# Expert outputs stored from ScalarE's DMA queue and read back in two sets, with eight extra products ahead of the combine

## The chip, the cores and the metric

The kernel runs on one core of a Trainium2 chip. The metric is the device time of one execution in microseconds: the median of three runs before the change is 980.36 us (977.6 to 984.06).

## The reference, cut to what matters

The program is a small vision tower: patch embedding of 64 images (37 tokens of 192 values each), causal linear attention, a soft mixture of 64 experts, a neighbourhood attention and a routed mixture of 8 experts. The change touches only the soft mixture. All of it is in 32-bit floats.

```python
d = softmax(logits, axis=tokens)            # dispatch weights, 64 experts, one slot each
c = softmax(logits, axis=experts)           # combine weights
xs = einsum('bmd,bmn->bnd', xn, d)          # one input row per image and expert
h  = gelu(einsum('bnd,ndh->bnh', xs, w1) + b1)   # w1: 64 x 192 x 768
ys = einsum('bnh,nhd->bnd', h, w2) + b2          # w2: 64 x 768 x 192
y  = einsum('bnd,bmn->bmd', ys, c)          # combine: every token mixes the 64 rows of its image
```

Each expert makes 64 rows of 192 values, one for each image. The combine needs, for a tile of three images, the rows of all 64 experts for these images.

## The kernel before

Five engines run five programs that meet at semaphores only. Within an engine, and within the DMA queue of an engine, all is issued in the written order. The stages follow each other: embedding, attention, dispatch, experts, combine, neighbourhood attention, routed experts. The experts and the combine are the place of the change.

**Experts.** The 64 experts are worked through as 32 pairs (expert p on output partitions 0 to 63, expert p + 32 on 64 to 127). For each pair SyncE's (SP's) queue loads two blocks of 1152 KB: w1 at L1067, w2 at L1070. They go into a ring of six places (`RING`; tiles `w1s`/`w1l` and `w2s`/`w2l`). TensorE (PE) makes the hidden product of pair s (L1177, L1181), the transposes of pair s - 1 (L1192) and the output product of pair s - 2 (L1203). ScalarE (ACT) copies half of the hidden rows (L1106, `copy_h`), applies gelu to the pair before (L1111), and copies the output of the pair before that into one of four tiles `eo` (L1118, `output`); VectorE (DVE) copies the other half and adds b1.

**Where the outputs go.** For the first 27 pairs (`DIRECT`) SP stores the two 64 x 192 halves of `eo` to `ys` in DRAM (L1078). These stores stand in the same queue as the loads: after the loads of pair p + 6. For pairs 27 to 31 SP copies from `eo` straight into the combine's tiles, one expert at a time (L1081, three transfers for an expert, each into one partition). Once the stores of pairs 0 to 26 have landed, six transfers of 27 rows each bring these back from DRAM (L1091, L1092).

**The combine's tiles.** They lie in ring places that are free by then: `e1` (in `w1l`) holds images 0 to 20 of expert n in partition n, and images 21 to 41 in partition 64 + n; `e2` (in `w2l`) holds images 42 to 63 in partition n, and b2 in partitions 64 to 127 (L1083, one load of 64 rows). A row of `e1` is 21 x 192 values (16,128 bytes), one of `e2` 22 x 192 (16,896 bytes). So in the trace L1091 reads as `w1l<-ys`, L1092 as `w2l<-ys`, and L1081 as `w1l<-eo` and `w2l<-eo`.

**Combine.** PE transposes the combine weights of 22 tiles (L1243, L1244), ACT copies them out (L1218), and then PE waits at L1248 for all rows of `e1` and `e2` before its 44 products (L1258, L1259). VectorE adds each to `h` (L1226). The next stage starts behind them.

Of the kernel before, what the change touches and what calls it, by code (L numbers as in the profile page):

```python
# [14 lines left out]
B, C_IN, IMG, PATCH = 64, 3, 96, 16  # L15
# [5 lines left out]
GB = 3  # L21
TP = GB * S
PARTS = ((0, TP // 16 * 16), (TP // 16 * 16, TP))
T = 22
# [4 lines left out]
NE, HID = 64, 768  # L29
HB = HID // 128  # L30
NPAIR = NE // 2
RING = 6
EARLY = 2
EOB = 4
DIRECT = 27
HALF_HID = HID // 2
QKW = 2 * NH * DH
VGW = NH * DH + ED
# [79 lines left out]
def tower(nc, ins, rows_out):  # L118
    with ExitStack() as ctx:
        scope = [ctx]  # L120

        def sb(name, shape, dt=F32):
            return scope[-1].enter_context(nc.sbuf_tensor(name, shape, dt))
# [9 lines left out]
        def sem(name):  # L133
            return ctx.enter_context(nc.semaphore(name))

        bank = [ctx.enter_context(nc.psum_tensor(f"bank{i}", [128, 512], F32)) for i in range(8)]
# [9 lines left out]
        ident = identity[:]  # L146
# [26 lines left out]
        xy = sb("xy", [128, 2, NE, B])  # L173
# [4 lines left out]
        w1s = [sb(f"w1s{q}", [128, 3 * HID]) for q in range(EARLY)]  # L178
        w2s = [sb(f"w2s{q}", [128, 2, HB, ED]) for q in range(EARLY)]
# [88 lines left out]
        eo = [sb(f"eo{b}", [128, ED]) for b in range(EOB)]  # L268
# [3 lines left out]
        e1 = w1l[:, 0:2].rearrange("p s (t d) -> p (s t) d", d=ED)  # L272
        e2 = w2l[:, 0:2].rearrange("p s e j d -> p (s e j) d")
        cTs = [w1l[:, 2:4].rearrange("p s n -> p (s n)"), w2l[:, 2].rearrange("p e j d -> p (e j d)")]

        def cT(t):
            k, at = t // CTN, t % CTN * 2 * TP
            return cTs[k][:, at:at + 2 * TP].rearrange("p (c q) -> p c q", c=2)
# [87 lines left out]
        ys_of = ys.rearrange("(n m) d -> n m d", n=NE)  # L366
# [60 lines left out]
        s_eoo = [sem(f"slot_output_out{b}") for b in range(EOB)]  # L427
# [18 lines left out]
        s_w1 = [sem(f"w1_in{q}") for q in range(RING)]  # L446
        s_w2 = [sem(f"w2_in{q}") for q in range(RING)]
        s_dh = sem("expert_hidden_product")
# [4 lines left out]
        s_dy = sem("expert_output_product")  # L453
        s_do = sem("expert_output_stored")
# [3 lines left out]
        s_el = sem("expert_rows_in")  # L458
# [45 lines left out]
        s_h = sem("h_updated")  # L504
# [552 lines left out]


        def experts_sp(sp):
            for s in range(NPAIR + RING):  # L1060
                q = s % RING
                if s < NPAIR:
                    if s == EARLY:
                        sp.wait_ge(s_h, 2 * T)
                    if s >= RING:
                        sp.wait_ge(s_dh, s - RING + 1)
                    sp.dma_start(w1s[q][:], ins["w1"][s]).then_inc(s_w1[q], 16)  # L1067
                    if s >= RING:
                        sp.wait_ge(s_dy, s - RING + 1)
                    sp.dma_start(w2s[q][:], ins["w2"][s]).then_inc(s_w2[q], 16)  # L1070
                p = s - RING
                if p >= 0:
                    b = p % EOB
                    sp.wait_ge(s_do, p + 1)
                    for e in range(2):
                        n = p + e * NPAIR
                        if p < DIRECT:
                            sp.dma_start(ys_of[n], eo[b][e * B:(e + 1) * B]).then_inc(s_eoo[b], 16)  # L1078
                        else:
                            for to, lo, hi in places(n):  # L1080
                                sp.dma_start(to, eo[b][e * B + lo:e * B + hi]).then_inc(s_eoo[b], 16)  # L1081
                if p == DIRECT:
                    sp.dma_start(e2[NE:2 * NE, 0:T], ins["b2"].rearrange("n (t d) -> n t d", d=ED)).then_inc(s_el, 16)  # L1083
                if p == DIRECT + 1:
                    for r in range(DIRECT - EOB, DIRECT):
                        sp.wait_ge(s_eoo[r % EOB], rows_out_by(r))
                    for k in range(2):
                        n = slice(k * NPAIR, k * NPAIR + DIRECT)
                        for g in range(2):
                            to = slice(g * NE + k * NPAIR, g * NE + k * NPAIR + DIRECT)  # L1090
                            sp.dma_start(e1[to, 0:T - 1], ys_of[n, g * (T - 1):(g + 1) * (T - 1)]).then_inc(s_el, 16)  # L1091
                        sp.dma_start(e2[n, 0:T], ys_of[n, 2 * (T - 1):B]).then_inc(s_el, 16)  # L1092

        def places(n):
            return ((e1[n:n + 1, 0:T - 1], 0, T - 1), (e1[NE + n:NE + n + 1, 0:T - 1], T - 1, 2 * (T - 1)), (e2[n:n + 1, 0:T], 2 * (T - 1), B))

        def rows_out_by(p):
            return sum(16 * (2 if r < DIRECT else 2 * GB) for r in range(p % EOB, p + 1, EOB))

        def experts_act(act):  # L1100
            def copy_h(p):
                b = p % 2
                act.wait_ge(s_dh, p + 1)
                if p >= 2:
                    act.wait_ge(s_dt, p - 1)
                nc.scalar.copy(eh[b][:, 0:HB // 2], hidden_bank(b, 0)).then_inc(s_dc[0], 1)  # L1106

            def gelu(p):
                b = p % 2
                act.wait_ge(s_db, p + 1)  # L1110
                nc.scalar.activation(eg[b][:], eg[b][:], ACT.Gelu).then_inc(s_dg, 1)  # L1111

            def output(p):
                b = p % 2
                act.wait_ge(s_dy, p + 1)
                if p >= EOB:
                    act.wait_ge(s_eoo[p % EOB], rows_out_by(p - EOB))
                nc.scalar.copy(eo[p % EOB][:], bank[6 + b][:, 0:ED]).then_inc(s_do, 1)  # L1118

            for s in range(NPAIR + 2):  # L1120
                if s < NPAIR:
                    copy_h(s)
                if 0 <= s - 1 < NPAIR:
                    gelu(s - 1)
                if s >= 2:
                    output(s - 2)

        def hidden_bank(b, part):
            return bank[2 * b + part][:, 0:HALF_HID].rearrange("p (j k) -> p j k", j=HB // 2)
# [104 lines left out]
        def combine_pe(pe):  # L1234
            for part in range(2):
                pe.wait_ge(s_dc[part], NPAIR)

            def transpose_c(t):
                pe.wait_ge(s_ecw, t + 1)
                if t >= 4:  # L1240
                    pe.wait_ge(s_eTa, t - 3)
                spread = cw[t % CB][:].rearrange("p g n -> p (g n)")
                nc.tensor.transpose(bank[t % 4][:, 0:TP], spread[:, 0:128], ident[0:TP, 0:TP])  # L1243
                nc.tensor.transpose(bank[t % 4][:, TP:2 * TP], spread[:, 128:4 * NE], ident[0:TP, 0:TP]).then_inc(s_eT, 1)  # L1244

            for t in range(T):
                transpose_c(t)
            pe.wait_ge(s_el, 16 * (1 + 2 * GB))  # L1248
            for b in range(EOB):
                pe.wait_ge(s_eoo[b], rows_out_by(NPAIR - EOB + b))  # L1250
            pe.wait_ge(s_db, NPAIR)
            pe.wait_ge(s_do, NPAIR)
            pe.wait_ge(s_eTa, T)

            def product(t):
                if t >= 4:
                    pe.wait_ge(s_h, 2 * T + t - 3)
                nc.tensor.matmul(bank[4 + t % 4][0:TP, 0:ED], cT(t)[:, 0], e1[:, t, :], start=True, stop=False)  # L1258
                nc.tensor.matmul(bank[4 + t % 4][0:TP, 0:ED], cT(t)[:, 1], e2[:, t, :], start=False, stop=True).then_inc(s_ey, 1)  # L1259

            for t in range(T):
                product(t)
# [738 lines left out]
        @block.sync  # L2001
        def _(sp):
            embed_sp(sp)
            sp.wait_ge(s_cbi, 32)
            experts_sp(sp)
            near_sp(sp)
            routed_sp(sp)
# [7 lines left out]
        @block.scalar  # L2015
        def _(act):
            embed_act(act)
            attention_act(act)
            dispatch_act(act)
            experts_act(act)  # L2020
            combine_act(act)
            near_act(act)
            near_act2(act)
            route_act(act)
            routed_act(act)
# [12 lines left out]
        @block.tensor  # L2038
        def _(pe):
            embed_pe(pe)  # L2040
            attention_pe(pe)
            dispatch_pe(pe)
            experts_pe(pe)
            combine_pe(pe)
            near_pe(pe)
            route_pe(pe)
            routed_pe(pe)
# [106 lines left out]
```

## Time and profile before

| | us |
|---|---|
| runs before | 977.6, 980.36, 984.06 |
| profiled execution, its own time | 982.76 |
| span from its first to its last instruction | 980.9 |
| experts, first hidden product to last output product | 263.4 to 436.6 |
| transposes of the combine weights | 436.5 to 442.2 |
| products of the combine | 458.5 to 475.6 |

The profiled execution lies 2.4 us above the median of the three runs and inside their range. Its mean granted TensorE clock is 0.912. TensorE is busy in 88% of the span; there is no second engine near that. The 16 DMA engines are 90% busy or more only in some stretches, and the longest of these is the experts' stage.

Times in all rows are microseconds from the start of the span, unless ns is written. "DMA share" is the mean busy share of the 16 DMA engines.

### The profile page before, as it was taken

The numbers are of one execution on the slowest core, as the hardware profiler recorded it, in microseconds if no ns is written. First come the engines' busy times: TensorE is split into PE (matmuls) and PEld (weight loads), VectorE is DVE, ScalarE is ACT, GpSimd is POOL, SyncE is SP. The second block draws the span as 40 slices with busy tenths as digits, with TensorE's granted clock in tenths as the row PEclk, the third lists the DMA queues.
The fourth block names the chain that finished last, engine by engine and source line by source line (L and its number), as shares of the span: only waits on it lengthen the run. The fifth ranks groups of instructions, "written<-read, shape, count | busy, mean of one in ns | idle before, by whom it ended". The sixth has DMA issues, their size and how long they took to land. (4 is left out here: it accounts for less than half of the span.)

```text
span 980.9 us, 17879 instructions
## 1 busy us (share of the span) xinstructions
PE 858.5 (88%) x6209; PEld 621.5 (63%) x6209; DVE 455.5 (46%) x1520; ACT 318.1 (32%) x904; POOL 280.1 (29%) x242
## 2 busy tenths in 40 slices
PE   6899999899999999893997999977465999999991
PEld 6787888676466655463854777757453666666661
DVE  6864565548443322241654688836781222222220
ACT  2544333237433332240042566633101121221210
POOL 1540000000000000000233455530027488888444
PEclk9999999799899999996997899985556999999996
DMA  8992000270089999982500000002005354455222
GB/s 265 281 329 97 2 2 2 81 305 2 23 320 423 423 422 423 425 263 70 175 1 1 1 2 0 1 2 53 24 24 140 79 105 104 92 101 104 39 24 25
DMA packets 59881, 128.93 MB, mean 131 GB/s; under 512 B 26334, under 2 KB 42256, under 8 KB 50112
## 3 DMA queue, kind: packets, MB, share of 16 engines
q1 hardware_dynamic: 29858, 118.61, 33.3%
q0 software_dynamic: 29952, 9.36, 7.0%
q8 instruction: 45, 0.74, 0.3%
q14 instruction: 26, 0.21, 0.1%
HBM read 115.76 MB, written 11.49 MB: 130 GB/s over the span
## 5 line engine op out<-in xcount | busy, mean ns | idle before, releaser
L1831 POOL DMA_INDIRECT out_dram<-yr,put x48 | 105.7, 2203 | 58.3 <-issue 35.4
L1286 POOL MEMSET xg<- 96x74 f32 x1 | 0.2, 157 | 406.9 <-PE bank L1259 406.9
L1818 POOL DMA_INDIRECT zr<-z_rows,take x48 | 66.6, 1388 | 84.6 <-issue 84.6
L1895 PE MATMUL bank<-zTa,w 128*128 128x372 f32 x256 | 90.0, 496 | 0.8 <-DVE zTb L1969 0.8
L1978 DVE TENSOR_TENSOR hT<-sg,bank 128x372 f32<-128x372 f32 x64 | 31.8, 538 | 107.5 <-ACT sg L1939 63.1
L1895 PEld LDWEIGHTS bank<-zTa,w 128*128 128x128 f32 x256 | 47.5, 194 | 38.2 <-ACT sg L1939 8.4
L1143 DVE COPY eh<-bank 128x384 f32<-128x384 f32 x32 | 17.8, 558 | 110.6 <-PE bank L1181 110.6
L1909 PE MATMUL bank<-w2r,hT 128*124 128x192 f32 x384 | 66.1, 329 | 0.8 <-DVE hT L1978 0.8
L1939 ACT ACTIVATE sg<-bank 128x372 f32<-128x372 f32 x64 | 27.3, 478 | 115.4 <-PE bank L1900 115.4
L1909 PEld LDWEIGHTS bank<-w2r,hT 128*124 128x124 f32 x384 | 61.9, 187 | 3.8 <-issue 3.8
L1327 POOL TENSOR_TENSOR nl<-nl,nr 111x1036 f32<-111x1036 f32 x22 | 42.1, 1914 | 61.7 <-DVE nr L1437 61.7
L1463 ACT ACTIVATE nl<-nl,nn 111x259 f32<-111x259 f32 x88 | 43.9, 500 | 48.1 <-DVE nn L1430 48.1
L1572 PE MATMUL bank<-kT,qx 96*111 (+1 forms) x176 | 53.5, 434 | 1.4 <-DVE nm L1428 1.3
L800 PE MATMUL bank<-wtok_c,xT 128*111 128x192 f32 x264 | 46.3, 331 | 5.7 <-DMA xT<-in_xT_dram 4.1
L1900 PE MATMUL bank<-zTb,w 64*128 64x372 f32 x256 | 48.7, 498 | 0.0
L800 PEld LDWEIGHTS bank<-wtok_c,xT 128*111 128x111 f32 x264 | 42.1, 176 | 9.9 <-issue 6.5
L1428 DVE CUSTOM_DVE_ANT_0 nl<-bank,bias 111x259 f32<-111x259 f32 x88 | 36.6, 424 | 15.4 <-issue 15.0
L1203 PE MATMUL bank<-w2l,eg 128*64 128x192 f32 x480 | 43.4, 330 | 0.0
L1111 ACT ACTIVATE eg<-eg 128x768 f32<-128x768 f32 x32 | 27.0, 845 | 41.0 <-DVE eg L1154 41.0
L1106 ACT COPY eh<-bank 128x384 f32<-128x384 f32 x32 | 15.3, 479 | 69.3 <-PE bank L1181 69.3
L1900 PEld LDWEIGHTS bank<-zTb,w 64*128 64x128 f32 x256 | 22.0, 186 | 24.6 <-issue 17.0
L1572 PEld LDWEIGHTS bank<-kT,qx 96*111 96x111 f32 x176 | 29.7, 195 | 12.0 <-issue 4.2
(298 smaller groups left out, 1798.4 us busy)
## 6 DMA issues: line engine op xcount, KB each, us to landing
w1l<-in_w_dram SPq DMA_DIRECT2D x20, 1152.0 KB, 16.3
w2l<-in_w_dram SPq DMA_DIRECT2D x20, 1152.0 KB, 16.9
w1s<-in_w_dram SPq DMA_DIRECT2D x12, 1152.0 KB, 15.5
w2s<-in_w_dram SPq DMA_DIRECT2D x12, 1152.0 KB, 15.1
w<-in_w_dram SPq DMA_DIRECT2D x8, 1024.0 KB, 8.0
xt<-in_x_dram SPq DMA_DIRECT2D x22, 336.0 KB, 8.0
xT<-in_xT_dram SPq DMA_DIRECT2D x22, 333.0 KB, 7.4
w2r<-in_w2r_dram SPq DMA_DIRECT2D x8, 384.0 KB, 4.1
```

The lines of the kernel that those rows point to most:

```text
L800: last = nc.tensor.matmul(bank[2 + q % 2][0:TP, 0:ED], xT[q][:, k, :], wtok_c[:, k, :], start=(k == 0), stop=(k == KC - 1))
L1203: last = nc.tensor.matmul(bank[6 + b][e * B:(e + 1) * B, 0:ED], eg[b][:, j, e, :], w2s[q][:, e, j, :], start=(j == 0), stop=(j == HB - 1))
L1327: nc.gpsimd.tensor_tensor(nl[q][:], nl[q][:], nr[b][:].unsqueeze(2).to_broadcast([TP, NHN, KW]), ALU.mult).then_inc(s_nw, 1)
L1428: nc.vector.tensor_tensor_reduce(nl[q][:, head, :], bank[1 + head % 2][0:TP, 0:KW], bias[v][:, head, :], 1.0, -3.0e38, ALU.add, ALU.max, n ...
L1463: last = nc.scalar.activation(nl[q][:, head, :], nl[q][:, head, :], ACT.Exp, bias=nn[b][:, head:head + 1], accum_out=nsum[b][:, head:head ...
L1572: nc.tensor.matmul(bank[1 + head % 2][0:TP, 0:KW], qx[q % 2][:, head, :], kT[:, bass.ds(first, KW)], start=True, stop=True).then_inc(s_nS, 1)
L1818: nc.gpsimd.indirect_dma_start(zr[b][:, j, :], None, z_rows, bass.IndirectOffsetOnAxis(ap=take[:, k:k + 1], axis=0), bounds_check=NROW - 1 ...
L1831: nc.gpsimd.indirect_dma_start(rows_out, bass.IndirectOffsetOnAxis(ap=put[:, k:k + 1], axis=0), yr[e % 2][:, j, :], None, bounds_check=OUT ...
L1895: nc.tensor.matmul(bank[to + 2 * part + half][:, 0:HS], w13[b][:, 0, at:at + 128], zTa[b][:, half * HS:(half + 1) * HS], start=True, stop= ...
L1900: nc.tensor.matmul(bank[to + 2 * part + half][:, 0:HS], w13[b][rows, 1, at:at + 128], zTb[b][rows, :], start=False, stop=True).then_inc(s_ ...
L1909: last = nc.tensor.matmul(bank[2 + j % 2][0:SP_, 0:ED], hT[:, m, j * SP_:(j + 1) * SP_], w2r[b][:, m, :], start=(m == 0), stop=(m == EH // ...
L1978: nc.vector.tensor_tensor(hT[:, m, half * HS:(half + 1) * HS], sg[half][:], bank[4 * (m % 2) + 2 + half][:, 0:HS], ALU.mult).then_inc(s_hT, 1)
```

## The change

Three things change. ACT issues the stores of all 32 pairs, each right behind its copy to `eo`, after waiting for that copy; SP issues no stores and no direct copies any more. SP reads the rows back in two sets of six transfers: pairs 0 to 27 (28 rows a transfer) and pairs 28 to 31 (4 rows a transfer), each set after a wait for the stores of its last four pairs; b2 is loaded once pair 27's output product is done. And PE issues eight products of the identity with 256 columns of `xy`, a tile that lies in SBUF already, between the transposes and its wait; their result is not used.

```diff
-DIRECT = 27
+FIRST = 27
...
         def experts_sp(sp):
-            for s in range(NPAIR + RING):
+            for s in range(NPAIR):
                 q = s % RING
...
+                if s == EARLY:
+                    sp.wait_ge(s_h, 2 * T)
+                if s >= RING:
+                    sp.wait_ge(s_dh, s - RING + 1)
+                sp.dma_start(w1s[q][:], ins["w1"][s]).then_inc(s_w1[q], 16)
+                if s >= RING:
+                    sp.wait_ge(s_dy, s - RING + 1)
+                sp.dma_start(w2s[q][:], ins["w2"][s]).then_inc(s_w2[q], 16)
+                if s == NPAIR - 1:
+                    sp.wait_ge(s_dy, FIRST + 1)
                     sp.dma_start(e2[NE:2 * NE, 0:T], ins["b2"].rearrange("n (t d) -> n t d", d=ED)).then_inc(s_el, 16)
...
+            for first, last in ((0, FIRST), (FIRST + 1, NPAIR - 1)):
+                for p in range(last + 1 - EOB, last + 1):
+                    sp.wait_ge(s_eoo[p % EOB], rows_out_by(p))
+                for k in range(2):
+                    read_back(sp, slice(k * NPAIR + first, k * NPAIR + last + 1))
+
+        def read_back(sp, n):
+            for g in range(2):
+                to = slice(g * NE + n.start, g * NE + n.stop)
+                sp.dma_start(e1[to, 0:T - 1], ys_of[n, g * (T - 1):(g + 1) * (T - 1)]).then_inc(s_el, 16)
+            sp.dma_start(e2[n, 0:T], ys_of[n, 2 * (T - 1):B]).then_inc(s_el, 16)
 
         def rows_out_by(p):
-            return sum(16 * (2 if r < DIRECT else 2 * GB) for r in range(p % EOB, p + 1, EOB))
+            return 32 * (p // EOB + 1)
...
                 nc.scalar.copy(eo[p % EOB][:], bank[6 + b][:, 0:ED]).then_inc(s_do, 1)
+                act.wait_ge(s_do, p + 1)
+                for e in range(2):
+                    act.dma_start(ys_of[p + e * NPAIR], eo[p % EOB][e * B:(e + 1) * B]).then_inc(s_eoo[p % EOB], 16)
...
-            pe.wait_ge(s_el, 16 * (1 + 2 * GB))
-            for b in range(EOB):
-                pe.wait_ge(s_eoo[b], rows_out_by(NPAIR - EOB + b))
+            for _ in range(8):
+                nc.tensor.matmul(bank[4][:, 0:256], ident, xy[:, 0, 0:4, :].rearrange("p n m -> p (n m)"), start=True, stop=True)
+            pe.wait_ge(s_el, 16 * (1 + 4 * GB))
```

ACT in the experts' steady state, one pair and the start of the next, before:

```order
L1106 COPY eh<-bank 128x384
L1111 ACTIVATE eg<-eg 128x768
L1118 COPY eo<-bank 128x192
L1106 COPY eh<-bank 128x384
L1111 ACTIVATE eg<-eg 128x768
```

and with the change:

```order
L1094 COPY eh<-bank 128x384
L1099 ACTIVATE eg<-eg 128x768
L1106 COPY eo<-bank 128x192
L1109 DMA ys<-eo 64x192 x2
L1094 COPY eh<-bank 128x384
```

Two DMA issues now stand on ACT between the output copy of one pair and the hidden copy of the next.

SP from the last loads to the end of the combine's transfers, before (from the stores of pair 26):

```order
L1078 DMA ys<-eo 64x192
L1081 DMA w1l<-eo 1x21x192 [waits expert_output_stored]
L1081 DMA w1l<-eo 1x21x192
L1081 DMA w2l<-eo 1x22x192
L1081 DMA w1l<-eo 1x21x192 x2
L1081 DMA w2l<-eo 1x22x192
L1083 DMA w2l<-in_b_dram 64x4224
...
L1091 DMA w1l<-ys 27x4032 [waits slot_output_out1,slot_output_out2,slot_output_out0,slot_output_out3]
L1091 DMA w1l<-ys 27x4032
L1092 DMA w2l<-ys 27x4224
```

and with the change (from the last load of w2):

```order
L1069 DMA w2s<-in_w_dram 128x2304 [waits expert_output_product]
L1072 DMA w2l<-in_b_dram 64x4224 [waits expert_output_product]
L1082 DMA w1l<-ys 28x4032 [waits slot_output_out2,slot_output_out3,slot_output_out1,slot_output_out0]
L1082 DMA w1l<-ys 28x4032
L1083 DMA w2l<-ys 28x4224
L1082 DMA w1l<-ys 28x4032 x2
L1083 DMA w2l<-ys 28x4224
L1082 DMA w1l<-ys 4x4032 [waits slot_output_out2,slot_output_out3,slot_output_out1,slot_output_out0]
L1082 DMA w1l<-ys 4x4032
L1083 DMA w2l<-ys 4x4224
```

The 30 direct copies of pairs 27 to 31 are gone from SP; six transfers of four rows, behind one more wait, take their place.

## Rows read from the trace of the kernel before

**Rows 1.** Waits of PE: waiter and releaser, total us, times, longest.
```profile
PE bank L1258 <- DMA w2l<-eo: 16.3, 1, 16.3
```

**Rows 2.** Windows: each engine's busy us and instructions, PEclk, DMA share, GB/s.
```profile
300.00:360.00 60.00, 60.00 (x554) 36.30 (x550) 19.29 (x37) 19.69 (x36) 0.00 (x0) 1.00 1.02 424
360.00:426.00 66.00, 57.63 (x510) 32.59 (x506) 17.38 (x33) 18.41 (x35) 0.00 (x0) 1.00 1.01 421
426.00:434.00 8.00, 7.67 (x74) 5.13 (x76) 2.60 (x5) 2.20 (x4) 0.00 (x0) 1.00 0.84 177
434.00:448.00 14.00, 8.19 (x74) 6.33 (x70) 4.79 (x14) 7.84 (x26) 0.00 (x0) 0.95 0.57 183
450.00:456.00 6.00, 0.00 (x0) 0.00 (x0) 0.00 (x0) 0.00 (x0) 0.00 (x0) 0.50 0.28 37
452.00:456.00 4.00, 0.00 (x0) 0.00 (x0) 0.00 (x0) 0.00 (x0) 0.00 (x0) 0.50 0.19 27
456.00:458.50 2.50, 0.00 (x0) 0.00 (x0) 0.00 (x0) 0.00 (x0) 0.00 (x0) 0.50 0.00 0
```

**Rows 3.** Timeline, one late pair: start, duration, engine, line [idle before <-releaser].
```profile
392.05 0.48 ACT L1106 COPY eh<-bank 128x384 f32<-128x384 f32 x1 [2.57 <-PE bank L1181]
...
393.88 0.84 ACT L1111 ACTIVATE eg<-eg 128x768 f32<-128x768 f32 x1 [1.35 <-DVE eg L1154]
...
394.94 0.32 ACT L1118 COPY eo<-bank 128x192 f32<-128x192 f32 x1 [0.21 <-PE bank L1203]
...
396.13 3.88 SPq L1078 DMA_DIRECT2D ys<-eo  x2
...
398.65 0.48 ACT L1106 COPY eh<-bank 128x384 f32<-128x384 f32 x1 [3.39 <-PE bank L1181]
...
400.06 0.64 SPq L1067 DMA_DIRECT2D w1s<-in_w_dram  x1
```

**Rows 4.** Line L1078, issue of one store: ns min/median/max, first and last start.
```profile
L1078 SPq DMA_DIRECT2D ys<-eo x54: 445/597/3665, 275.5 to 414.7; - x54
```

**Rows 5.** Timeline from the last stores to the combine's first product.
```profile
408.39 6.89 SPq L1078 DMA_DIRECT2D ys<-eo  x4
...
424.79 0.55 SPq L1083 DMA_DIRECT2D w2l<-in_b_dram  x1
425.29 0.32 ACT L1118 COPY eo<-bank 128x192 f32<-128x192 f32 x1 [0.21 <-PE bank L1203]
...
433.26 0.68 SPq L1091 DMA_DIRECT2D w1l<-ys  x2
...
436.60 0.32 ACT L1118 COPY eo<-bank 128x192 f32<-128x192 f32 x1 [1.78 <-PE bank L1203]
...
441.93 0.26 PE L1244 MATMUL bank<-identity,cw 111*128 111x111 f32 x1
...
449.07 0.77 SPq L1081 DMA_DIRECT2D w2l<-eo  x1
458.50 0.44 PEld L1258 LDWEIGHTS bank<-w1l 128*111 128x111 f32 x2 [16.53 <-issue]
```

**Rows 6.** DMA issues: tiles, queue, count, KB each, median us to landing.
```profile
w1l<-ys SPq DMA_DIRECT2D x4, 425.2 KB
...
w2l<-ys SPq DMA_DIRECT2D x2, 445.5 KB
...
z_rows<-zk SPq DMA_DIRECT2D x1, 67.5 KB, 3.2
```

**Rows 7.** Windows of the combine, columns as in Rows 2.
```profile
446.00:450.00 4.00, 0.00 (x0) 0.00 (x0) 0.00 (x0) 0.00 (x0) 0.00 (x0) 0.58 0.48 151
458.50:462.00 3.50, 3.47 (x11) 3.39 (x12) 0.91 (x3) 0.00 (x0) 0.00 (x0) 0.50 0.00 0
462.00:464.00 2.00, 2.00 (x9) 1.95 (x8) 0.75 (x4) 0.00 (x0) 0.00 (x0) 0.57 0.00 0
```

**Rows 8.** Line L1002, earlier products of the identity with 256 columns: ns min/median/max.
```profile
L1002 PE MATMUL bank<-w1s,identity x60: 379/379/741, 190.0 to 215.0; 128*128 128x256 f32 x60
```

More of the change, by code:

```diff
@@ L1059, in experts_sp @@
         def experts_sp(sp):
-            for s in range(NPAIR + RING):
+            for s in range(NPAIR):
                 q = s % RING
[L1062 to L1082, printed above, removed]
-                    sp.dma_start(e2[NE:2 * NE, 0:T], ins["b2"].rearrange("n (t d) -> n t d", d=ED)).then_inc(s_el, 16)
[L1084 to L1092, printed above, removed]
@@ L1094, in places @@
-        def places(n):
-            return ((e1[n:n + 1, 0:T - 1], 0, T - 1), (e1[NE + n:NE + n + 1, 0:T - 1], T - 1, 2 * (T - 1)), (e2[n:n + 1, 0:T], 2 * (T - 1), B))
+                if s == EARLY:
[6 more added lines that the diff above has]
+                sp.dma_start(w2s[q][:], ins["w2"][s]).then_inc(s_w2[q], 16)
```

## The prediction

> **What bounds the kernel now.** I read the waits of PE first, because PE is busy almost all the time and what it waits for is what can be saved. One wait belongs to this change: 16.3 us before the combine's first product, for transfers into the combine's tiles [rows 1]. Next I read the windows by stage [rows 2]. From 300 to 426 us the DMA engines are at a share of 1.01 to 1.02 and move 421 to 424 GB/s. From 360 us on PE is busy in only 57.63 of 66 us while the DMA engines never rest: the loads of the expert weights set the pace there. After 426 us the picture turns round. The DMA share falls to 0.57 and the rate to 183 GB/s, then to 37 and 27 GB/s, and 2.5 us without any DMA pass before PE starts. So the end of the stage is set by a chain of transfers that are slow without filling the engines. The timeline has its links [rows 5]: the last stores of pairs up to 26 are issued by 415.3 us (408.39 + 6.89), SP issues the read-back at 433.26, the last output is copied at 436.60 to 436.92, SP issues its last direct copy at 449.07, PE starts at 458.50. PE has had nothing to do since 442.2 (441.93 + 0.26).
>
> **Loads: no gain.** SP loses an issue of 3.88 us for each pair's stores [rows 3], and the next w1 load can be issued that much earlier. But the bytes of loads and stores up to 426 us stay the same, and at a share of 1.01 an earlier issue only lengthens the queue. I take 0. If the share fell below 1 there, this would be a gain of at most the 8.4 us that PE stands idle between 360 and 426 us (66 - 57.63) [rows 2]; nothing in the rows points to that.
>
> **ACT: no cost, with a limit.** ACT now issues two stores after each output copy and waits for that copy first. No row has a DMA issued by ACT. The nearest is the same store on SP: 0.445 us at least, 0.597 median, 3.665 at most [rows 4]. So a pair costs ACT 0.9 to 7.3 us. I take the median, 1.2, since the high values come when SP's own queue is full of loads, and ACT's queue holds none. What waits behind it is the next hidden copy, and ACT is idle for 3.39 us before that [rows 3]. Over 360 to 426 us ACT is idle 47.6 us (66 - 18.41) [rows 2]; at 6.6 us a pair (398.65 - 392.05) [rows 3] that is ten pairs and 4.7 us a pair. So 1.2 us is covered, and up to 4.7 us could be. At the end, ACT's issue for pair 31 delays its copies of the combine weights by 1.2 us, so the transposes end near 443.4. PE waits much longer than that.
>
> **First set.** Pair 27's output copy ends at 425.61 [rows 5]; the two issues end at 426.8. Landing: the low end is 3.2 us, a lone store of similar size [rows 6]; the high end is 18 us, what lies between the last stores' issue at 415.3 and the read-back that waited for them at 433.26 [rows 5], behind loads. I take 5 us, near the low end because no load stands ahead in ACT's queue, but the engines are still at 0.84 [rows 2] with the last loads and b2. With about 1 us for issue and first bytes, the set runs from 433: where it ran before. It is 28/27 of 4 x 425.2 + 2 x 445.5 KB [rows 6], that is 2,688 KB or 2.75 MB. At 183 GB/s [rows 2] that is 15.0 us, to 448. The low end: a share of 0.57 is 9.1 engines, and 27 rows can be dealt evenly to nine; if 28 rows go to fourteen at the same 20 GB/s an engine, 9.8 us. I take 15.0, since b2 with 64 rows shows that more engines need not mean more bytes: 177 GB/s at a share of 0.84 [rows 2].
>
> **Second set.** It waits for pair 31's stores: copied at 436.92 [rows 5], issued at 438.1, landed between 441.3 (3.2 us) and 456.1 (18 us). I take about 448, because they share the engines with the first set; so the set starts at about 448.5, behind the first. Its six transfers have 4 x 16,128 or 4 x 16,896 bytes, together 393 KB. Four rows can be dealt to four engines only, which is my inference from the nine above. The low end is four engines at the load stage's pace (424/16 = 26.5 GB/s each): 3.7 us. The high end is the slowest stretch of the direct copies, 27 GB/s [rows 2]: 14.6 us. I take 37 GB/s [rows 2], 10.6 us, because those copies too write to very few partitions at a time, and so are nearest to four. That ends at 459.1.
>
> This is where a rule of the Trainium skill speaks against the change. The rows show that transfers into few partitions are slow for the engines they keep busy: 27 GB/s at a share of 0.19 is 9 GB/s an engine, against 26.5 in the loads [rows 2]. The page SBUF — State Buffer, section Door 1: The DMA port swizzle, says that bandwidth depends on how many of 16 ports the partitions reach, at about 27.2 GB/s each, and puts partitions 28 to 31 and 60 to 63 on one port. By that page the second set takes about 14.5 us where the sum has 10.6; the trace's 27 GB/s for single partitions agrees.
>
> **The eight products.** At 0.379 us each [rows 8] they last 3.0 us, from 443.4 to 446.4, and delay nothing. The clock fell at 446.6 before (a mean of 0.58 over 446 to 450 [rows 7]), 4.4 us after PE went idle at 442.2, and the combine began at half of 2.4 GHz: 0.50, then 0.57 up to 464 [rows 7]. That costs about 2.6 us, half of the first 5.2. With the start that I get, PE is idle for some 15 us behind the eight products; the clock falls all the same. I take 0, with a gain of 2.6 if the gap stays shorter than it was when the clock fell.
>
> **Sum.** 459.1 plus 2.5 us from the last bytes to PE [rows 2] is 461.6, against 458.5: +3.1 us, and all later stages shift with it. The profiled execution of 982.76 us becomes about 986. It lies 2.4 us above the median of 980.36, so for a median I forecast 980.4 + 3.1, 983.5, and round to **984 us**.
>
> **Rivals.**
> - *Faster: the second set is not slow.* All low ends at once: first set from 431 to 440.8, second from 441.8 to 445.5, PE at 448.0, 10.5 us earlier, and 2.6 more from the clock, since PE then idles only 1.6 us: about 967. For it: no more single-partition copies, fourteen engines instead of nine. Against it: the low rates after 426 us, in three kinds of transfer. Half way, with the first set at 15 us and the second at 3.7, PE starts at about 455, 4 us earlier. Chance 0.17, of which 0.08 over 1%.
> - *The rows go one transfer after another at the slowest rate.* Second set 14.6 us, PE at 465.6, +7.1: about 987. It is the skill's rule, told above. Chance 0.12.
> - *Slower: pair 31's stores land late.* If they take 18 us, as the last stores did before, they land at 456.1, the set runs from 456.6 to 467.2, PE starts at 469.7, +11.2: about 992. For it: ACT issues them while the engines work through the first set's long rows. Against it: the 18 us came behind loads. It costs over 1% from a landing of 16.6 us on; below 9.9 us it costs nothing beyond the forecast. Chance 0.16.
> - *Slower: ACT's issues are held up in the loads.* From 4.7 us a pair on, ACT becomes the bound; at 7.3 us it is 2.6 us a pair over some ten pairs, +26: about 1010. Chance 0.05.
> - *The eight products do not do what they are there for.* This is inside the forecast: without a gap under 4.4 us the clock is as before.
>
> **Numbers.** The forecast, +3.1 with its own range of -3 to +9 us (977 to 989), has chance 0.50. About 1%, or 9.8 us, is what a measurement of this kernel can tell from no change. Faster by over 1%: 0.08. Slower by over 1%: 0.15 from the late landing, 0.05 from ACT, together 0.20. Within: 0.72. The range of 970 to 994 reaches half of the fast case and the late landing, and leaves out ACT's and the full fast case.
>
> **What would show it.** The loads' DMA share stays at 1.0 up to about 426 us and PE's hidden products keep their spacing: the loads' step is right. ACT's idle time before the hidden copy shrinks by about 1.2 us; if it goes to zero in most pairs, ACT's step was wrong. The first 28-row transfer is issued near 432, the first 4-row one between 441 and 449. In the stretch of the second set the rate is 27 to 40 GB/s; if it is over 80, the faster rival holds. PE's first combine product stands near 461, at a granted clock of 0.50. The prediction is wrong above all if the rate of the second set is, or if the stores on ACT's queue land much sooner or later than I took.

## The result: 0.45% slower, as forecast in size, by terms that missed in both directions

| | before | after |
|---|---|---|
| median of 15 runs each, us | 984.38 (977.6 to 987.67) | 988.31 (983.14 to 992.18) |
| ratio, with 95% interval | | 1.0045 (1.0026 to 1.0064) |
| profiled execution, its own time | 982.76 | 988.92 |
| span | 980.9 | 987.1 |
| ACT's last output copy to the combine's first product | 436.60 to 458.53: **21.93** | 435.74 to 460.71: **24.97** |

The kernel became 4.4 us slower (0.0045 x 984.4; 2.6 to 6.3). The forecast was +3.1 us and 984 us. 4.0 of the 4.3 us between 984 and 988.31 lie in the base: 15 runs of the kernel before have a median of 984.38, the three that the forecast began from had 980.36. So 988.31 is still inside the forecast's own 977 to 989, by 0.7 us. The last line of the table is the change's own price in the profile: +3.04 us. Everything below is measured in this distance, because the stage itself begins earlier or later from one execution to the next: the first hidden product stands between 258.0 and 268.6 us in the profiles of this document.

**The profile after.** PE's wait into the combine, as waiter and releaser, total us, times, longest; it answers [rows 1]. The releaser is now the second read-back (`w2l<-ys`):

```profile
PE bank L1249 <- DMA w2l<-ys: 14.9, 1, 14.9
```

The windows, columns as in [rows 2]: the load stage, the first set, the second set, and the combine's beginning.

```profile
300.00:360.00 60.00, 59.62 (x550) 35.98 (x544) 19.29 (x37) 19.38 (x36) 0.00 (x0) 1.00 1.02 423
360.00:426.00 66.00, 58.15 (x512) 32.94 (x514) 17.37 (x33) 18.36 (x34) 0.00 (x0) 1.00 1.02 422
...
434.00:448.00 14.00, 10.68 (x82) 8.65 (x78) 4.87 (x14) 7.16 (x24) 0.00 (x0) 1.00 0.83 196
446.00:450.00 4.00, 0.00 (x0) 0.00 (x0) 0.00 (x0) 0.00 (x0) 0.00 (x0) 0.93 0.16 43
...
450.10:459.90 9.80, 0.00 (x0) 0.00 (x0) 0.00 (x0) 0.00 (x0) 0.00 (x0) 0.50 0.22 40
460.70:466.00 5.30, 5.29 (x17) 5.14 (x18) 1.60 (x5) 0.00 (x0) 0.00 (x0) 0.50 0.00 0
```

Up to 426 us nothing has changed: share 1.02, 422 GB/s, the same PE load. From 434 to 448 us the share rose from 0.57 [rows 2] to 0.83, 13.3 engines on average (0.83 x 16) in place of 9.1, but the rate only from 183 to 196 GB/s. In the second set some four engines (0.22 x 16 is 3.5) move 40 GB/s: by the packet records (the trace has start, length and size of every DMA packet) its 24 rows run from 450.18 to 459.90 us, 9.7 us. The clock fell and PE begins the combine at 0.50, as before.

The timeline of a late pair, answering [rows 3]: start, duration, engine, line, [idle before <-releaser].

```profile
386.24 0.48 ACT L1094 COPY eh<-bank 128x384 f32<-128x384 f32 x1 [2.57 <-PE bank L1172]
...
389.12 0.32 ACT L1106 COPY eo<-bank 128x192 f32<-128x192 f32 x1 [0.21 <-PE bank L1194]
389.47 1.70 ACTq L1109 DMA_DIRECT2D ys<-eo  x2
...
392.02 0.48 ACT L1094 COPY eh<-bank 128x384 f32<-128x384 f32 x1 [2.58 <-PE bank L1172]
```

The two issues lie inside the 2.58 us in which ACT waits for PE anyway; these hidden copies follow each other at 5.78 us.

The timeline from the first set's issue to the combine, answering [rows 5]:

```profile
431.70 0.77 SPq L1082 DMA_DIRECT2D w1l<-ys  x2
...
435.74 0.32 ACT L1106 COPY eo<-bank 128x192 f32<-128x192 f32 x1 [1.95 <-PE bank L1194]
...
436.08 1.10 ACTq L1109 DMA_DIRECT2D ys<-eo  x2
...
442.15 3.63 PE L1240 MATMUL bank<-xy,identity 128*128 128x256 f32 x16
...
449.32 0.58 SPq L1082 DMA_DIRECT2D w1l<-ys  x2
...
460.71 0.98 PE L1249 MATMUL bank<-w1l 128*111 128x192 f32 x2 [14.92 <-DMA w2l<-ys]
```

SP issues the second set at 449.32, when pair 31's stores have landed: 12.1 us after ACT finished issuing them (436.08 + 1.10). The DMA issues from 428 to 461 us (KB each, median us from issue to landing; [rows 6] has those of before) say the same of the last six stores:

```profile
ys<-eo ACTq DMA_DIRECT2D x6, 48.0 KB, 11.8
```

The span grew by 6.2 us, 3 more than the distance. Before the tail the profile after is 0.9 us ahead, so the other 4 us arise behind the combine, in stages that the change doesn't touch. The windows of the neighbourhood attention show a part of them: before,

```profile
545.00:550.00 5.00, 4.97 (x22) 3.87 (x21) 2.77 (x13) 2.92 (x10) 2.13 (x2) 0.60 0.00 0
550.00:556.00 6.00, 5.84 (x60) 4.74 (x61) 4.24 (x24) 3.32 (x12) 2.38 (x2) 1.00 0.00 0
```

and after:

```profile
545.00:550.00 5.00, 5.00 (x22) 4.40 (x22) 2.81 (x14) 2.16 (x9) 1.30 (x2) 0.50 0.02 3
550.00:556.00 6.00, 6.00 (x37) 4.38 (x36) 3.09 (x18) 2.28 (x9) 2.13 (x2) 0.57 0.00 0
```

The clock came back near 549 before (a mean of 0.60 over 545 to 550) and near 555 after (0.57 over 550 to 556), 4 us more than the stage is late, and 37 products were done where 60 had been. In the granted-clock records this stretch at 0.50 lasts 27.3 us here (527.9 to 555.2), 23.9 us before (525.2 to 549.0), and 23.9 us again in the first and the eighth experiment, which have the same two sets. So nothing ties it to the change; it is most likely of this one execution. The ratio's interval covers 3.1 us without it.

### The profile page after: what moved, and what is told of

Same layout as the page of the kernel before. It is cut to its first block and busy times, and to the rows that moved or that the text cites. A ratio compares the mean times of both kernels' runs of the same rounds, so it can differ in the third digit from the quotient of the medians.

```text
span 987.1 us, 17897 instructions
## 1 busy us (share of the span) xinstructions
PE 865.5 (88%) x6225; PEld 626.6 (63%) x6225; DVE 455.4 (46%) x1520; ACT 318.0 (32%) x904; POOL 279.8 (28%) x242
## 5 line engine op out<-in xcount | busy, mean ns | idle before, releaser
L1930 ACT ACTIVATE sg<-bank 128x372 f32<-128x372 f32 x64 | 27.3, 478 | 115.6 <-PE bank L1891 115.6
```

## The experiments

Each distance is from the start of ACT's last output copy to the combine's first product, as in the table above; the expectations count from the end of the last output product, 0.04 us earlier. Ratios are to runs of the kernel before on the same chip; these had medians of 985.17, 984.45 and 985.76 us in the three groups of runs (1 to 4, 5 to 8, 9 to 11). My theory after the result: the chain is pair 31's stores, then a second set slow because it writes to few partitions; the products do nothing. The main rivals: the stores' place on ACT costs something by itself, and the read-back is limited by all engines together, wherever it writes.

**1. Without the eight products.**

```diff
-            for _ in range(8):
-                nc.tensor.matmul(bank[4][:, 0:256], ident, ...)
```

> The changed kernel without the eight products of the identity. Theory (the second set's chain sets the start of the combine, the clock falls with or without the products): the combine's first product stays at 460.7 us, within 0.5, after 15 us of waiting without the products' 3.6 us, again at a granted clock of 0.50; against the kernel before the ratio stays at 1.0045, within 0.003. Rival (the products hold something up, or keep the clock for part of the combine): the time moves by 2 us or more against the changed kernel.

Ratio 1.0026 (1.0 to 1.0053); 442.26 to 466.73, 24.47 us. The products neither cost nor gain anything that can be seen. The first product itself stands at 466.73 us and not at 460.7, because the whole stage began 5.9 us later.

**2. Only the stores moved to ACT.** The kernel before, with the stores of pairs 0 to 26 issued by ACT; direct copies and the read-back of 27 rows stay on SP.

```diff
...
                 nc.scalar.copy(eo[p % EOB][:], bank[6 + b][:, 0:ED]).then_inc(s_do, 1)
+                if p < DIRECT:
+                    act.wait_ge(s_do, p + 1)
+                    for e in range(2):
+                        act.dma_start(ys_of[p + e * NPAIR], ...)
```

> The kernel before with one part of the change: ACT issues the stores of pairs 0 to 26, the direct copies of pairs 27 to 31 and the one read-back of 27 rows stay on SP. Theory (the loads are bound by the DMA engines, so an earlier issue gives nothing; only the end of the stage counts): the last output product ends where it did, 436.6 us within 1; the read-back is issued some 1 to 3 us earlier than at 433.3, and the combine starts 0 to 3 us before 458.5; ratio 0.997 to 1.0. Rival (ACT's issues or a second queue cost the loads something): the last output product ends later by 2 us or more and the time is above that of before.

Ratio 0.9993 (0.997 to 1.0016); 440.99 to 461.63, 20.64 us: 1.3 us less than before. The last output product ends at 440.95 and not at 436.6, which was the rival's first sign; but the first hidden product is 4.7 us later too, and from one to the other the experts take 172.9 us (173.2 before). The time is not above that of before, so the rival is out. The move to ACT alone is free. With the first run, which leaves out the products, the 3 us come from what becomes of the last pairs and of the read-back.

**3. One set.** All 32 rows are read back behind pair 31's stores.

```diff
-            for first, last in ((0, FIRST), (FIRST + 1, NPAIR - 1)):
+            for first, last in ((0, NPAIR - 1),):
```

> The changed kernel with a single read-back of all 32 rows, issued once pair 31's stores have landed: 3.1 MB in place of the second set's 0.39 MB at the end. Theory (rows into few partitions are slow, and 32 rows spread over eight times as many partitions run at the rate of the first set, about 196 GB/s, so eight times the bytes cost less than twice the time): pair 31's stores land within 5 us as nothing else moves then (441 to 443), the read-back takes 15 to 16 us, and the combine starts at 459 to 461, the same as with two sets; ratio 1.001 to 1.006. Rival A (bytes over the engines' full rate count): 3.1 MB at 424 GB/s take 7.4 us, and the combine starts near 452. Rival B (the second set's rate holds per byte, 0.39 MB in 8.7 us): the combine starts far later, beyond 500.

Ratio 0.9973 (0.9951 to 0.9994); 437.07 to 456.58, **19.51 us**: 5.5 less than with two sets, and 2.4 less than before. The timeline, and the DMA issues from 428 to 461 us:

```profile
437.42 1.10 ACTq L1109 DMA_DIRECT2D ys<-eo  x2
439.98 1.53 SPq L1082 DMA_DIRECT2D w1l<-ys  x2
...
456.58 0.98 PE L1249 MATMUL bank<-w1l 128*111 128x192 f32 x2 [9.46 <-DMA w2l<-ys]
```

```profile
ys<-eo ACTq DMA_DIRECT2D x6, 48.0 KB, 2.4
```

```profile
442.00:454.00 12.00, 5.12 (x30) 4.12 (x28) 0.91 (x3) 3.40 (x10) 0.00 (x0) 0.84 1.02 229
```

With no read-back beside them the same six stores land in 2.4 us (median) where they took 11.8, and pair 31's within 1.5 us of their issue (438.52 to 439.98). So reading back early is what delays the stores that the second set waits for. The expectation of 459 to 461 missed this by 2.4 us, by 3.8 us counted from the last copy: it gave the stores up to 5 us, and they took 1.5. And 3.1 MB take 14.9 us (440.95 to 455.84 by the packet records), where the 0.39 MB of the second set alone took 9.7.

**4. One set from two queues.** As the third, but ACT issues the two transfers into partitions 64 to 127.

```diff
-            for g in range(2):
-                sp.dma_start(e1[to, 0:T - 1], ...)
+            sp.dma_start(e1[n, 0:T - 1], ...)
...
+                act.dma_start(e1[to, 0:T - 1], ys_of[n, T - 1:2 * (T - 1)])
```

> As the single read-back of 32 rows, but the two transfers into partitions 64 to 127 are issued by ACT, the four into partitions 0 to 63 by SP, at the same time. Theory (each half of the partitions has its own limit near 100 to 110 GB/s per 32 rows' worth of time, and one queue works through its transfers one after another, so only one half is busy at a time): both halves run together, the read-back takes the time of four transfers of the six, about 10 us, and the combine starts at 453 to 456; ratio 0.996 to 1.0. Rival (the limit is the DRAM side or all engines together at about 196 GB/s): two queues change nothing, 15 to 16 us, start at 459 to 461.

Ratio 0.9955 (0.9929 to 0.9981); 436.29 to 455.59, 19.30 us. The start at 455.6 lies inside what the theory expected, but not for its reason: the read-back took 14.9 us (440.16 to 455.10 by the packet records), as long as from one queue, and not the 10 us that it wanted. So a second queue gains nothing here, and no run shows a limit of 100 to 110 GB/s for each half. What does limit the rows is left open by this run: of the first 128 rows 63 are ACT's, so both halves were written at once, but the records do not name the engine of a row. (ACT waits for the last stores before it copies the combine weights, so the transposes end at 446.93; PE waits longer than that.)

**5. One set, rows spread over the partitions.** Row 32k + i moves from partition 64g + 32k + i to 4i + 2k + g, so that a transfer reaches every fourth partition and not 32 neighbours. b2 follows, in two transfers, and DVE spreads the combine weights in two operations a tile.

```diff
-                to = slice(g * NE + n.start, g * NE + n.stop)
-                sp.dma_start(e1[to, 0:T - 1], ...)
+                sp.dma_start(e1[rows_of(n, g), 0:T - 1], ...)
...
+        def rows_of(n, g):
+            k, first = n.start // NPAIR, n.start % NPAIR
+            at = 4 * first + 2 * k + g
+            return slice(at, at + 4 * (n.stop - n.start - 1) + 1, 4)
```

> One read-back of all 32 rows behind pair 31's stores, as in the run with one set, but row 32k+i of the combine lies in partition 4i+2k+g instead of 64g+32k+i, so that each of the six transfers reaches partitions across all 128 and not 32 neighbours (b2 in two transfers; VectorE's spread of the weights in two operations a tile). Measured with the rows in neighbouring partitions: last output to first combine product 19.55 us, read-back 14.9 us at 1.16 us a row. Theory, that the few neighbouring partitions are what slows the rows: a row near 0.62 us, the load stage's 26 GB/s an engine, the read-back near 7.5 us, last output to first product near 12 us, ratio 0.987 to 0.991. Rival, that all 16 engines together move no more than about 210 GB/s in this transfer wherever it writes: rows of 1.16 us, read-back 14.9 us and 19.5 us as before, ratio 0.997.

Ratio 0.9923 (0.9891 to 0.9955); 431.20 to 445.27, **14.07 us**, 5.4 less than in neighbouring partitions. The windows of the read-back's middle and of the combine's beginning:

```profile
438.00:444.00 6.00, 4.31 (x21) 3.32 (x20) 0.50 (x3) 2.32 (x4) 0.00 (x0) 1.00 0.93 365
445.30:446.00 0.70, 0.70 (x4) 0.70 (x5) 0.00 (x0) 0.00 (x0) 0.00 (x0) 0.96 0.00 0
446.00:449.00 3.00, 3.00 (x12) 2.90 (x11) 1.10 (x4) 0.00 (x0) 0.00 (x0) 0.50 0.00 0
```

The same bytes from the same rows of DRAM, again on some 16 engines: 24.5 GB/s an engine (365 / (0.93 x 16)) in place of 14.0 (229 / (1.02 x 16)); of the read-back only the partitions that it goes to differ. The rival is out. The gain is 2 us smaller than expected: the read-back took 9.6 us (435.37 to 444.95) and not 7.5. By the packet records most rows take 0.60 to 0.63 us, but 29 of the 192 take more than 0.8, the first ones about 1.1, and the mean is 0.68.

Of this the Trainium skill's page SBUF — State Buffer, section Door 1: The DMA port swizzle, states that 32 neighbouring partitions reach 8 of 16 ports, about 218 GB/s, and all 128 reach 16; the measured 229 GB/s (a little above it) and 365 GB/s agree in kind.

**6. Two sets, rows spread**: the changed kernel with the fifth run's edit.

> The changed kernel with the combine's rows spread over the partitions in steps of 4. Measured in the changed kernel: last output to first combine product 25.0 us, pair 31's stores land 12 us after their issue, the second set runs 8.7 us. Theory, few neighbouring partitions: first set in about 7 to 8 us, so that pair 31's stores find the engines free and land within 5 us; second set near 4 us; last output to first product 11 to 14 us, ratio 0.985 to 0.990. Rival, limit independent of the partitions: 24 to 26 us and 1.004, as changed.

Ratio 0.9942 (0.9908 to 0.9976); 440.00 to 457.14, 17.14 us. Windows of the first and of the second set:

```profile
434.00:447.00 13.00, 11.67 (x107) 8.79 (x104) 7.62 (x30) 7.75 (x25) 0.00 (x0) 1.00 0.86 224
451.00:456.80 5.80, 0.21 (x1) 0.00 (x0) 0.00 (x0) 0.00 (x0) 0.00 (x0) 0.86 0.21 68
```

Half right: 7.8 us less than the changed kernel, and the second set's rows run from 451.44 to 456.79 us by the packet records, 5.4 us in place of 9.7; but the first set stayed at 224 GB/s, 13 us, against 7 to 8 expected, and the last stores waited for it again (median landing of the eight from 428 us on 8.8 us). 17.14 us misses the expected 11 to 14.

**7. The sixth without the eight products.**

> The run with two sets and spread rows, without the eight products of the identity. If the theory of the partitions holds, PE's gap behind the last transposes is about as short as the time in which the clock still stood in the kernel before (4.4 us after PE went idle), and the eight products could decide whether the combine begins at 2.4 GHz. If they keep the clock: without them granted clock 0.50 at the combine's first products and 2 to 3 us longer than with them, ratio between the two near 1.0025. Rival, that they decide nothing (gap short enough, or too long in both): the same within 0.5 us, the clock at the first combine product the same in both.

Ratio 0.995 (0.9915 to 0.9985); 434.47 to 451.64, 17.17 us, and 0.50 at the combine's beginning in both. The rival holds: PE rested 5.9 us with the products and 9.4 without, both too long.

**8. The second set twice.** The changed kernel, with the six transfers of four rows issued once more behind the whole read-back.

```diff
+            sp.wait_ge(s_el, 16 * (1 + 4 * GB))
+            for k in range(2):
+                read_back(sp, slice(k * NPAIR + FIRST + 1, k * NPAIR + NPAIR))
```

> The changed kernel with the second set's six transfers (393 KB) issued once more behind the whole read-back, nothing else in flight: the price of this set alone. Theory, that a set of 4 rows is slow in itself because four neighbouring partitions take it in: the repeat adds about the 8.7 us of the second set plus 2 to 3 us from its wait to the first bytes, 11 us. Rival, that the second set was slow because it ran beside the last rows of the first and behind SP's issues: the repeat takes 3.7 us (four engines at 26.5 GB/s) and adds about 6 us.

996.23 us in one run; 435.55 to 471.95, 36.40 us: +11.4, as the theory had it. The window of the repeat:

```profile
461.00:471.00 10.00, 0.00 (x0) 0.00 (x0) 0.00 (x0) 0.00 (x0) 0.00 (x0) 0.50 0.20 39
```

Nothing else is in flight, and the repeat's rows run from 461.54 to 471.18 us by the packet records: 9.6 us, as long as the second set itself (9.7). The second set is slow in itself.

**9. Two spread sets, both behind pair 31's stores.**

```diff
-            for first, last in ((0, FIRST), (FIRST + 1, NPAIR - 1)):
-                for p in range(last + 1 - EOB, last + 1):
-                    sp.wait_ge(s_eoo[p % EOB], rows_out_by(p))
+            for p in range(NPAIR - EOB, NPAIR):
+                sp.wait_ge(s_eoo[p % EOB], rows_out_by(p))
+            for first, last in ((0, FIRST), (FIRST + 1, NPAIR - 1)):
```

> Two sets with rows spread over the partitions, but both are issued only behind pair 31's stores, so that nothing else is in flight. Measured: with two sets and spread rows, the first set issued beside the last stores, its rows take 1.0 us on 14 engines (13 us in all), last output to first product 17.2 us; with one set of 32 spread rows 0.62 to 0.7 us on 16 engines, 14.1 us. Theory, 28 rows dealt two to each of 14 engines are slow in themselves, even spread: rows near 1.0 us, first set 13 us, 19 to 21 us to the first product. Rival, the stores beside them slowed the rows: 0.62 to 0.75 us, first set 8 to 9 us, 14 to 16.5 us to the first product.

981.75 us in one run; 437.32 to 458.67, 21.35 us. The window of the first set's middle:

```profile
443.00:453.00 10.00, 5.33 (x26) 3.74 (x25) 1.64 (x7) 3.14 (x7) 0.00 (x0) 0.96 0.88 233
```

With no stores beside them 28 spread rows still go at 16.5 GB/s an engine (233 / (0.88 x 16)), where 32 go at 24.5. So the stores were not what slowed the first set of the sixth run. What does, in 28 rows on some 14 engines (0.88 x 16), stays open: the trace does not say which partitions are written at the same moment.

**10 and 11. The fifth with fourteen products of the identity, and with none.**

```diff
-            for _ in range(8):
+            for _ in range(14):
```

> One read-back with spread rows, and fourteen products of the identity in place of eight. Measured with eight: they end 2.8 us before the combine's first product, the clock falls 0.7 us into the combine and stands at 0.50 for 3.4 us, which costs 1.7 us. At 0.454 us each fourteen last 6.4 us and end near the combine's start. Theory, that it is PE's rest that lets the clock fall: 1.00 throughout the combine, 1.7 us less from first to last combine product, ratio to before 0.990 to 0.992. Rival, that these products of 256 columns do not count for the clock: it falls within the fourteen or just behind them, no gain, or a loss of up to 0.5 us where they delay the first product.

> One read-back with spread rows and no product of the identity. PE then rests some 6.5 us between the last transpose and the combine, longer than the 4.4 us after which the clock fell in the kernel before. Theory, the eight products kept part of the clock: without them 0.50 at the combine's first product and 4.5 to 5.2 us at that level, 0.6 to 0.9 us longer through the combine than with eight; ratio to before 0.992 to 0.994. Rival, that they only moved the fall later: the same 3.4 us at 0.50 and the same length of the combine.

Fourteen: ratio **0.9878** (0.9846 to 0.9909), 432.30 to 446.58, 14.28 us; the combine's products then last 14.55 us (446.58 to 461.13). None: 0.9887 (0.9851 to 0.9923), 14.61 us and 16.15 us; with eight they lasted 16.24. PE's products and the windows of the clock, with fourteen:

```profile
439.89 6.22 PE L1250 MATMUL bank<-xy,identity 128*128 128x256 f32 x28
446.58 0.58 PE L1259 MATMUL bank<-w1l 128*111 128x192 f32 x2 [0.46 <-DMA w2l<-ys]
```

```profile
446.50:448.00 1.50, 1.42 (x9) 1.43 (x10) 0.35 (x1) 0.00 (x0) 0.00 (x0) 1.00 0.00 0
448.00:452.00 4.00, 4.00 (x26) 4.00 (x25) 3.71 (x12) 0.00 (x0) 0.00 (x0) 1.00 0.03 6
```

and with none:

```profile
446.00:448.80 2.80, 0.00 (x0) 0.00 (x0) 0.00 (x0) 0.00 (x0) 0.00 (x0) 0.50 0.38 162
448.80:451.00 2.20, 2.16 (x7) 2.10 (x8) 0.35 (x1) 0.00 (x0) 0.00 (x0) 0.50 0.00 0
451.00:453.00 2.00, 2.00 (x11) 1.97 (x10) 0.95 (x4) 0.00 (x0) 0.00 (x0) 0.72 0.00 0
```

Fourteen bridge PE's rest but for 0.46 us, the clock stays at 1.00 (2.4 GHz), and the combine is 1.7 us shorter, as the theory had it. Eight are worth nothing here: with a rest of 2.8 us behind them the clock still fell 0.7 us into the combine and stood at 0.50 for some 3.4 us (446.0 to 449.4), as long as without them. So for fourteen the theory holds, and for eight the rival, that they only move the fall later. The three intervals overlap; that fourteen beat none is shown by the profiles, not by the times, and both ratios came out below what was expected of them (0.990 to 0.992, 0.992 to 0.994).

The version with fourteen has the lowest ratio of all: 972.7 us median, 1.2% under the kernel before. Its interval lies wholly below that of the changed kernel (1.0026 to 1.0064).

## Why the prediction was right, point by point

**Loads: right.** The share stays at 1.02 and 422 to 423 GB/s; from the first hidden product to the last output product the experts take 173.0 us after and 173.2 before. The issue saved on SP's queue, ahead of full engines, was worth nothing here.

**ACT: right.** A pair's two issues took mostly 1.1 us (forecast 1.2), and the second experiment with this part alone is no slower than before. The 6.6 us a pair, and the 3.39 us of idle time, were read from one long pair; most late pairs of before follow each other at 5.78 us with 2.57 us idle, so the room for the issues was smaller than told, and still enough. The extreme case of 26 us never came near: over the 64 stores one issue took 0.452 us at least, 0.556 median and 1.747 at most.

**First set: right.** Issued 431.70 (forecast 432), 196 GB/s at a share of 0.83 (forecast 183), last rows at 448.39 (forecast 448). That more engines need not mean more bytes was read from one line of before, b2's 177 GB/s at 0.84 [rows 2], and is what decided this term.

**Pair 31's stores: the mechanism right, the size 2.2 us short.** Counted from the last output copy they were to land after 11.4 us (436.6 to 448), and the second set was issued after 13.6 us (435.74 to 449.32). So the first transfer of four rows, at 449.32, just missed the 441 to 449 that was named as a sign. The stated reason, that they share the engines with long rows, is shown by the third experiment.

**Second set: slow as forecast, by a price that was partly luck.** Its rows took 9.7 us at 40 GB/s, against 10.6 at 37. The eighth experiment shows that it is slow by itself, the fifth and sixth that the place of the rows is one cause. The low end of 3.7 us would have held only with four engines at the loads' pace. But the 37 GB/s came from transfers of another kind. The direct copies went into one partition each, as the forecast said, and also in packets of 768 bytes, which it did not see. The packets from 450 to 456 us before, and from 450 to 460 us after:

```profile
DMA packets 332, 0.22 MB, mean 37 GB/s; under 512 B 94, under 2 KB 329, under 8 KB 329
```

```profile
DMA packets 48, 0.39 MB, mean 39 GB/s; under 512 B 24, under 2 KB 24, under 8 KB 24
```

Before, 329 of 332 packets are under 2 KB; after, the 24 that are not are rows of 16 KB. No run separates what small packets cost from what few partitions cost in the direct copies, so that the two rates lie so close is not shown to have one cause.

**From the last bytes to PE: 0.8 us, not 2.5** (459.90 to 460.71). The 2.5 us too were read behind the direct copies. In every run that ends on rows from DRAM this distance is 0.3 to 0.8 us; why the direct copies had more is open.

**The sum: luck in part.** The misses are +2.2 us on the stores, +0.4 from the issue to the first bytes (0.9 us, not 0.5), -0.9 on the second set and -1.7 behind it. They cancel: +3.04 in place of +3.1. The order of events was right; that the size is right to 0.1 us is not owed to the terms.

**The rule of the Trainium skill.** The prediction made 14.5 us of it for the second set, and took the trace's 27 GB/s of the direct copies as agreement. The set took 9.7 us, and 9.6 when alone, at more than 27.2 GB/s: the transfers do not follow one another at one port's rate, which is what the 14.5 takes. The table of the Trainium skill's page SBUF — State Buffer, section Door 1: The DMA port swizzle, has partitions 28 to 31 and 60 to 63 on one port, and 92 to 95 and 124 to 127, where two of the six transfers go, on another. The four transfers that share a port have 264 KB, which at the Trainium skill's 27.2 GB/s is an estimate of 9.7 us, and both measured totals agree with it. So the rate of a port held, as far as a total can tell, and one transfer after another did not; no run shows the port of a row. The 27 GB/s of before cannot be taken as agreement, since those packets were small.

**The products: right that they gain nothing,** 3.63 us in place of 3.0; each is two instructions (the row has x16), 0.454 us together. The price that went with them did not hold: the forecast gave 2.6 us for a rest shorter than the 4.4 us after which the clock fell before. In the fifth run the clock fell all the same with a rest of 2.8 us, and where it stayed, in the tenth, that was worth 1.7 us.

**Rivals.** "The second set is not slow" fails at 40 GB/s, against the 80 named as its sign. "The slowest rate", 14.6 us, fails at 9.7. "Pair 31's stores land late" came a quarter of the way: 13.6 us after the last output copy, against 11.4 forecast and 19.5 in the rival (436.6 to 456.1). That the mechanism exists made the rival worth naming; its size, from the 18 us of before behind loads, was too high.

**What the prediction did not see** is that the whole order was avoidable: it priced two sets against the kernel before, and not against one. Waiting for all stores and reading back once is 5.5 us shorter than the change, because the early set holds up the stores (third run) and leaves a tail for four engines (eighth). The ninth run adds, for spread rows, that two sets cost 7.3 us more than one even where no stores are in the way (21.35 against 14.07).

## What to carry to other kernels

Look at the DMA share and the GB/s of a window together: here a high share at a low rate (1.02 at 229 GB/s) came from the place that the rows were written to, and spreading them over every fourth partition was worth as much (5.4 us) as undoing the two sets (5.5 us). Look at the size of the packets before you take a rate from one kind of transfer for another. A transfer started early is not free when what it shares the engines with is on the path: beside the early set the last stores took 12.1 us in place of 1.5. Of the products meant to keep the clock, fourteen, which ended 0.5 us before the next work, gained 1.7 us; eight, which ended 2.8 us before it, gained nothing.

## What was not expected of the hardware

- Two stores of 48 KB land in 1.5 us on idle engines and in 12 us beside a read-back with rows of 16 KB.
- Spreading the rows of each transfer in steps of 4 partitions took the read-back of 32 rows from 229 to 365 GB/s, but with 28 rows on some 14 engines it went at 233 GB/s. The cause of the second is not settled.
- The clock fell after PE had already been at work again for 0.7 us, behind a rest of 2.8 us.
